# Constant products in TensorE's waits, and a logits product four times as wide

## The reference

```python
# 1. cross attention, 16 heads of 16, over a context of 1601 rows for each of 32 batches
q = layernorm(x) @ Wq.T + bq;  k = ctx @ Wk.T + bk;  v = ctx @ Wv.T + bv
x = x + (softmax(q @ k.T * 4) @ v) @ Wp.T + bp
# 2. the circuit layer
h = layernorm(x)
x1 = layernorm(h + cumprod(cos(h)))             # per head of 16
q = cumprod(cos(x1[..., :16]))
x = x + layernorm(x1 + relu(q @ w1.T + b1) @ w2.T + b2)
# 3. a shared expert and 7 routed ones, the best 2 for each token
h = layernorm(x)
p = softmax(h @ wr.T + rb)                      # the logits: 7 columns
x = x + expert(h, shared) + sum of the two best, weighted by p
```

## Time and profile before

| | us |
|---|---|
| median of 3 runs | 1988.65 |
| lowest and highest | 1985.05, 1988.9 |
| the profiled execution, its time | 1982.46 |
| the profiled execution, span from first to last instruction | 1980.4 |
| TensorE busy | 1889.5 (95%) |
| VectorE busy | 1475.0 (74%) |
| ScalarE busy | 1142.1 (58%) |
| mean granted TensorE clock | 0.975 |

### The profile page before, as it was taken

How to read it: one execution, slowest core, us unless ns; L and a number is a source line. 1 busy time by engine, 2 the same in 40 slices (tenths; PEclk the granted TensorE clock), 3 DMA queues, 4 the chain that set the end, 5 groups by cost and what they waited for, 6 DMA issues and landing times. The chain is left out here.

```text
span 1980.4 us, 46642 instructions
## 1 busy us (share of the span) xinstructions
PE 1889.5 (95%) x18834; PEld 1785.0 (90%) x18834; DVE 1475.0 (74%) x2801; ACT 1142.1 (58%) x1924; POOL 635.6 (32%) x616
## 2 busy tenths in 40 slices
PE   7899999999999999999999999999639889999998
PEld 5899999999999999999999999999527789999998
DVE  6777787777877777777777778777477567666666
ACT  2566656665665665665666566566565535666652
POOL 3222323222232322222322223320021135888860
PEclk9999999999999999999999999999968799999999
DMA  8666657666666666666666666665130435666634
GB/s 270 167 159 163 171 147 181 161 155 159 173 155 173 162 156 162 153 177 167 162 157 161 160 164 163 177 154 130 35 134 26 156 112 191 218 222 225 223 114 132
DMA packets 152613, 318.24 MB, mean 161 GB/s; under 512 B 58016, under 2 KB 83488, under 8 KB 148944
## 3 DMA queue, kind: packets, MB, share of 16 engines
q1 hardware_dynamic: 147024, 301.26, 56.0%
q0 software_dynamic: 4224, 11.54, 1.9%
q10 hardware_dynamic: 1152, 2.47, 0.5%
HBM read 136.49 MB, written 20.58 MB: 79 GB/s over the span
## 5 line engine op out<-in xcount | busy, mean ns | idle before, releaser
L288 ACT COPY a_pT<-a_pst 128x512 f32<-128x512 f32 x768 | 421.2, 583 | 413.2 <-PE a_pst L595 413.2
L294 ACT ACTIVATE a_probs<-a_probs,a_nmax 128x1601 f32<-128x1601 f32 x256 | 418.8, 1636 | 140.1 <-DVE a_probs L379 139.6
L379 DVE TENSOR_SCALAR_CACHE_REDUCE a_probs<-a_pss 128x1608 f32<-128x1608 f32 x256 | 467.3, 1826 | 14.8 <-PE a_pss L584 13.8
L595 PE MATMUL a_pst<-a_id,a_probs 128*128 128x128 f32 (+1 forms) x3328 | 450.9, 274 | 12.0 <-ACT a_pT L288 9.3
L595 PEld LDWEIGHTS a_pst<-a_id,a_probs 128*128 128x128 f32 (+1 forms) x3328 | 381.2, 140 | 49.8 <-issue 21.5
L249 POOL TENSOR_TENSOR a_tick<-a_tick 128x1 f32<-128x1 f32 x62 | 12.0, 194 | 950.9 <-DMA a_raw<-in_ctxT 916.1
L397 DVE TENSOR_SCALAR a_khi<-a_psk,a_bk 128x402 fp32r<-128x402 f32 x250 | 158.5, 634 | 142.8 <-PE a_psk L549 141.1
L254 POOL TENSOR_TENSOR a_clo<-a_raw,a_chi 128x402 fp32r<-128x402 f32 x240 | 247.1, 1061 | 4.8
L584 PE MATMUL a_pss<-a_kst,a_bd 96*128 96x402 f32 x1024 | 240.9, 357 | 5.2 <-DVE a_v L404 5.2
L547 PE MATMUL a_pso<-a_whi,a_chi 128*128 128x256 f32 (+1 forms) x806 | 241.2, 299 | 0.0
L549 PE MATMUL a_pso<-a_whi,a_clo 128*128 128x256 f32 (+1 forms) x806 | 226.6, 281 | 0.0
(11 more groups left out here) (239 smaller groups left out, 3524.0 us busy)
## 6 DMA issues: line engine op xcount, KB each, us to landing
a_kst<-a_khi SPq DMA_DIRECT2D x1008, 100.5 KB, 2.6
a_kst<-a_klo SPq DMA_DIRECT2D x504, 100.5 KB, 2.6
a_raw<-in_ctxT SPq DMA_DIRECT2D x60, 804.0 KB, 5.5
e_gur<-in_wgu SPq DMA_DIRECT2D x24, 1408.0 KB, 9.1
e_dr<-in_wd SPq DMA_DIRECT2D x24, 768.0 KB, 9.3
a_bd<-q_scr SPq DMA_DIRECT2D x192, 32.0 KB, 2.0
e_big<-ys_scr SPq DMA_DIRECT2D x8, 512.0 KB, 7.5
a_pT<-in_ctxT SPq DMA_DIRECT2D x2, 1608.0 KB, 8.9
```

The costliest lines, as they stand in the source:

```text
L288: nc.scalar.copy(pT[:, p % HALF, 4 * i:4 * i + 4, :], ps_t[:, i % 2, :].rearrange("p (t q) -> p t q", q=P)).then_inc(t_copied_act, 1)
L294: nc.scalar.activation(pr, pr, ACT.Exp, bias=nmax[:, b, p:p + 1], scale=-1.0, accum_out=esum[:, b, p:p + 1]).then_inc(probs_ready, 1)
L379: nc.vector.tensor_scalar(probs[:, p % 2, :].rearrange("p (b k) -> p b k", b=QK), ps_s[:, :, 0:KQ], -SCALE, None, ALU.mult, ALU.min, accum ...
L595: mm = nc.tensor.transpose(ps_t[0:r, i % 2, (t % 4) * P:(t % 4 + 1) * P], probs[:, p % 2, t * P:t * P + r], id_sb[:])
```

## The change

TensorE gets a helper, idle_work, which multiplies constants that are already in SBUF into a bank that nobody reads before its next real product. It is called:

- at the start of the prologue, once the block-diagonal tile is zeroed: 10 products of 512 columns, one pass
- behind the 15 steps of batch 0, ahead of the wait for their copies: 14 products of 512 columns, one pass
- in the last batch, behind the scores of six of the eight pairs and ahead of the wait for the exponential: 2 products of 512 columns each time, 12 in all
- in the circuit layer, 8 fp32 products of 256 columns as soon as group 0's variance is there, 2 more when group 0's angles are there, and one fp32 product of 128 columns ahead of each expand that directly follows an expand (34 of the 48)
- in the experts, 5 fp32 products of 256 columns ahead of turn_rows of block 0 and 3 behind it

The logits product writes each tile's 7 columns four times over (WIDE is 28): the moving operand repeats the router's weights, and VectorE reads the first 7 of 28. No other engine's list of instructions changes.

```diff
+WIDE = 4 * E
...
+            def idle_work(out, n, a, b):
+                for _ in range(n):
+                    nc.tensor.matmul(out, a, b, start=True, stop=True)
...
+            pe.wait_ge(bd_zeroed, 2)
+            idle_work(ps_s[:, 0, :], 10, bd[:, 0, 0, :], bd[:, 0, 0:4, :].rearrange("r p q -> r (p q)"))
             pe.wait_ge(wq_loaded, 48)
             turn_rows(0)
...
+            idle_work(ps_o[:], 14, w_hi[:, 0, 0, 0:P], w_hi[:, 0].rearrange("p k d -> p (k d)"))
             pe.wait_ge(kv_copied, STEPS)
...
                             scores(b, p)
+                            if last and b == 1:
+                                idle_work(ps_k[:], 2, w_hi[:, 0, 0, 0:P], w_hi[:, 0].rearrange("p k d -> p (k d)"))
                             pe.wait_ge(probs_ready, g)
...
-            nc.vector.tensor_tensor(lg[:], ps_l[:, 0:NT * E].rearrange("p (t e) -> p t e", e=E), rb_sb[:].unsqueeze(1).to_broadcast([P, NT, E]),
+            nc.vector.tensor_tensor(lg[:], ps_l[:, 0:NT * WIDE].rearrange("p (t e) -> p t e", e=WIDE)[:, :, 0:E], rb_sb[:].unsqueeze(1).to_broadcast([P, NT, E]),
...
-            for stage, g in PE_ORDER:
+            pe.wait_ge(var_done[1], 1)
+            idle_work(ps_l[:, 0:D], 8, id_sb[:], w2_sb[:, 0, :])
+            pe.wait_ge(q_angle, 1)
+            idle_work(ps_l[:, 0:D], 2, id_sb[:], w2_sb[:, 0, :])
+            for at, (stage, g) in enumerate(PE_ORDER):
+                if stage == "expand" and PE_ORDER[at - 1][0] == "expand":
+                    idle_work(ps_l[:, 0:P], 1, id_sb[:], w2_sb[:, 0, 0:P])
...
-                            mm = nc.tensor.matmul(ps_l[:, i * E:(i + 1) * E], xT[:, g % 4, NC * j + k, :], wr_sb[:, k, :], start=(k == 0), stop=(k == NC - 1))
+                            mm = nc.tensor.matmul(ps_l[:, i * WIDE:(i + 1) * WIDE].rearrange("p (w e) -> p w e", e=E), xT[:, g % 4, NC * j + k, :],
+                                                  wr_sb[:, k, :].unsqueeze(1).to_broadcast([P, WIDE // E, E]), start=(k == 0), stop=(k == NC - 1))
...
+            idle_work(ps_y[:, 0, 0:D], 5, id_sb[:], d_raw[:, 1, 0, :])
             turn_rows(0, 0)
+            idle_work(ps_y[:, 0, 0:D], 3, id_sb[:], d_raw[:, 1, 0, :])
```

## The result

The changed kernel takes 1998.87 us (median of six runs, 1995.68 to 2004.47), the kernel before 1987.92 (six runs beside them, 1985.05 to 1988.9). The ratio is 1.0059, with a 95% interval of 1.0042 to 1.0077: slower by 11 us between the medians, where 6 us less were forecast and 1990 was the upper end of the range. The profiled execution took 1998.2 us with a span of 1996.3, which is 15.9 more than before's. One execution differs from the next by several us, above all in the long attention part (from its first transposes to the last weighing of the values, 1362.9 us in one trace of this study and 1367.0 in another), so I compare stages and not spans.

The account below looks back on a forecast made before the run. TensorE was taken to bound the long middle, so only the edges' low clock could be won. Terms -0.4 (last batch) and -5.5 (circuit layer), others 0, sum to -5.9: 1988.65 - 5.9 = 1982.7 us, range 1977 to 1990.

Parts of the forecast that it names:

- The products between expands: Circuit layer: 0.23 us each at the high clock, covered in long runs, paid in five short ones, 1.2 us.
- The term -6.7 + 1.2 = -5.5: Circuit layer, the main term: 6.7 us won by a high clock, 1.2 us paid for products between expands.
- The clock at 1.00 through the layer: Circuit layer: clock at 1.00 from about 1460 to 1555 us, all eight contracts at 7.2 us.
- The size of the gain, given a high clock: Circuit layer: gains capped by ScalarE's and VectorE's waits, 2.5, 3.2, 4.2 and finally 6.7 us.
- The start of the layer: Circuit layer up to group 1's contract: the first 10 products raise the clock; 3.2 us offered, at most 2.5 taken.
- rival A: Circuit layer: clock rises early but falls in the runs of expands; -1 to -4, say 1986; chance 0.22.
- The prologue: Before the dense stretch at 61.00: 24 products covered by TensorE's waits, worth 0, range 0 to +1.7 us.
- The last batch: End of attention, 12 products: 0.6 us won by preventing the clock's fall, 0.2 lost; -0.4, ends +0.2 and -0.6.
- The wide logits: End of circuit layer: 28 columns cost 0 and doubtfully hold the clock; 0, ends 0 and -1.0 us.
- The experts' start: Eight products around turn_rows: gain at most 1.4 us, loss some 0.7, taken as 0 since the clock ends low.
- D: Slower: constant products run at the low clock and stand in TensorE's way; +7 us, 1996; chance 0.08.

Follow-up runs that it names:

- e13: Kernel before, with expands of 96 rows (48 new rows of zeros): 1981.02 us, ratio 0.9978.
- e1: Changed kernel without the 34 products between expands: 1985.83 us, ratio 1.0000.
- e2: Changed kernel with the 34 products between expands made one-pass, 48 rows by 512 columns: 1988.07 us, ratio 1.0005.
- e4: Changed kernel with the 34 products between expands still fp32 with 128 columns, but on 48 rows: 1986.56 us, ratio 0.9998.
- e5: Changed kernel with the 34 fp32 products between expands on 64 rows: 1986.27 us, ratio 0.9998.
- e14: Changed kernel with expands of 96 rows, all its products as they are: 1977.62 us, ratio 0.9955.
- e16: Changed kernel with expands of 96 rows, without the prologue's 24 products and the 34 between expands: 1981.08 us, ratio 0.9971.
- e12: Changed kernel without the prologue's 24 products, the fp32 products between expands in twos behind every second expand: 1984.26 us, ratio 0.9995.
- e15: Changed kernel with expands of 96 rows and without the prologue's 24 products: 1976.15 us, ratio 0.9956.
- e9: Kernel before with only the 10 early products of the prologue added: 1984.61 us (one run).
- e7: Changed kernel with the 34 products between expands made one-pass, 128 rows and 96 columns: 1992.80 us, ratio 1.0035.
- e10: Kernel before with only the prologue's 14 products ahead of the first scores added: 1989.44 us (one run).

## Why the prediction was wrong

**The products between expands** are the step that failed. The forecast priced one at 0.23 us from the 7-column and the 256-column record and called it covered in the long runs. Both rows are of records that stand among their like; the price held for the record and not for the place between two expands, where the two seams of 0.2 us come on top. The hint was in the trace of before: a contract's last record, two expands of 256 columns and the step to the transposes take 0.74 us from 1545.69 to 1546.43, for 0.22 + 2 x 0.11 = 0.44; e13, with expands of 96 rows, has 0.45 there (1543.06 to 1543.51). TensorE in that stretch, before:

```profile
1545.69 0.38 PE L1045 MATMUL f_psf<-f_w,f_hT 128*128 128x256 f32 x1
1546.00 0.50 PE L1035 MATMUL f_psh<-f_qT,f_w 48*128 48x256 f32 x2
1546.43 0.66 PE L1055 MATMUL f_psx<-f_id,f_a 128*128 128x128 f32 x4
```

I had costed the sum of the records and not the distance of the starts. That 128 columns cost no more than 7 does hold for records among their like: in the kernel before the four transposes at 1556.54 and the logits behind them at 1556.98 are 0.11 us apart, the 7-column records 0.114. The 34 were to cost 1.2 us of the layer and cost 15.7 (151.2 in the changed kernel, 135.5 without them). The term -6.7 + 1.2 = -5.5 measured +13.5.

**The clock at 1.00 through the layer** failed as well, and would have kept the forecast from coming true even without the seam. In the changed kernel the clock fell three times in the runs of expands (at 1468.5, 1489.0 and 1526.5, 10 us each). Of the -6.7 us e1's layer shows -2.2, and e2, e4 and e5, where the 34 stand without a seam, have layers of 136.1 to 139.4 us and the time of the kernel before. So of the 19.0 us between -5.5 and +13.5, 14.5 are the seam (15.7 for 1.2) and 4.5 the clock (-2.2 for -6.7).

**The size of the gain, given a high clock,** was right, and e14 against e13, with expands of 96 rows in both, shows it term by term. Forecast: 2.5 taken at group 1's contract, 3.2 at the next, 4.2 at VectorE's step behind it, 6.7 less 1.2 = 5.5 in the end. Measured, from the layer's start to the contract in e13 less the same in e14: 2.5 at the second contract, 3.1 at the third, 3.3 at the fifth, 5.2 at the sixth and at the last logits. The caps read from ScalarE's and VectorE's waits fit, but for the 4.2, which is 0.9 more than measured; each number is of one trace on either side.

**The start of the layer** alone gives little (0.6 us in e16 against e13, 2.2 in e1 against before, neither far beyond the scatter of a layer): the clock rises early and falls in the first run of expands, which was rival A's mechanism.

**The prologue**, 0 with an end at +1.7: +1.6 at the first transposes, and another 1.4 by the scores that start at 69.68 us before and at 72.66 now, with the clock low from 62.2 to 65.6 (the records of the value projection are 0.21 us apart there, 0.12 before). The second part cannot be laid on the products: e12, e13, e15 and e16 have none in the prologue and run at the low level until 64.1 to 64.7, while e1 with all 24 is at the high one from 60.2 on. The end was too near, and the reason of the first part was another than I gave: I had called the ten early products covered by looking at the projection at 24.66, which indeed did not move, and not at SyncE's queue.

**The last batch**, -0.4, measured -0.57: the number is right, and by luck. From the third last weighing of the values to the last it takes 37.25 us before and 36.68 now. But it takes 36.71 and 36.69 in e9 and e13, which have no products there and no fall of the clock either, and in seven of the 13 traces with the products (e2, e4 to e7, e12, e16) the clock fell there all the same, for 37.30 to 37.77 us. No run shows that the products prevent the fall.

**The wide logits**: 28 columns cost nothing (32 records in 3.65 us, 3.64 before), right, and did not hold the clock, which was 0.50 from 1577.7 to 1591.4, also as said. The weight loads fill that time with either width, 3.65 us for the 32 before and after (PEld, L1062 and L1082). The last 8 records take 1.91 us at the low level (1.87 before), 0.24 each for 0.114 at the high one.

**The experts' start**, 0: right in the number, and the layer did end at the low level, as the forecast had it. turn_rows comes 0.8 us later behind the logits and the rank sums 1.5 earlier, and none of it arrives, since the plan waits for the end of GpSimd's subtracts and not for TensorE alone, which the forecast's cap of 1.4 us did not have. In no trace with these products is the way from VectorE's logits step to its first sum of expert results shorter than in the kernel before (29.08 to 31.45 us for 29.06; without them it varies too, up to 30.30 in e10).

**The rivals.** D came nearest in size (1996) and named the place, but for half of the reason: it needed the low level, where a pair of 512 columns was to take 0.88. It takes 0.85 at the high one and 1.45 at the low one (1491.00 to 1492.45), where the clock stood for 31 us of the expand runs and contracts.

## What to carry to other kernels

Before putting a product between others, compare its rows with theirs: here a matmul of 48 rows and one of 96 or 128 did not follow each other for free on TensorE (0.37 us for there and back at the high level), while 48 and 64 did (0.36 us from expand to expand, as with 48 and 48), and a run that alternated paid at every step. Price an instruction by the distance between starts at the place where it will stand, with its neighbours, not by its record among its like. Where a kernel has small contractions between large ones, filling them up with rows of zeros can win time: here, from 48 to 96 rows, two expands with a product between them start 0.36 us apart as with 48 (e14, e4), and the kernel before won 0.2% (e13, 0.9978). A gain read from one pair of traces, as in the last batch, needs a kernel without the edit that shows the same stage unchanged.

## What the runs showed of the hardware

- Going from a product of 48 rows to one of 96 or 128 and back costs 0.37 us at the high level and 0.59 at the low one (128 rows); 48 to 64 rows and one pass to two passes cost nothing that shows (0.36 us for an expand of 256 columns and an fp32 product of 128 in e4 and e5).
- In the attention the step from a transpose of 128 columns to the weighing with 32 takes 0.20 us where transposes are 0.11 apart. TensorE in the kernel before:

```profile
700.71 0.27 PE L602 MATMUL a_pst<-a_id,a_sc 128*128 128x128 f32 x1
700.91 3.05 PE L615 MATMUL a_pso<-a_pT,a_v 128*32 128x128 f32 x104
```

  No run here changed the columns of the weights, so what sets this step is not shown.
- Expands of 96 rows take as long as those of 48: 0.36 us to the next one across a product, in e14 as in e5.
- The clock stayed high for 92 us in a layer with many short waits with one short product of 128 rows between expands of 96 (e14, e15), fell two or three times where these gaps were empty (e13, e16), and fell three times with products of up to 64 rows between expands of 48 (e2, e4, e5).
